# Halves on GpSimd, a ring for XW, and the roots, x's parts and row sums moved in a two-layer graph kernel

## The reference

```python
N, D = 2708, 128                      # nodes, features; adj is a 0/1 matrix
# layer 0
deg = jnp.clip(adj.sum(axis=1), 1.0);  dis = deg ** (-0.5)
diffusion = (dis[:, None] * adj * dis[None, :]) @ x - x
sim = x @ x.T / (norms[:, None] * norms[None, :])
attn = softmax(beta * sim * adj, axis=1)
x = layernorm(x + diffusion + sigmoid(alpha) * (attn @ x - x))
# layer 1
XW = x @ W;  s_col = XW @ a[0, :D];  s_row = XW @ a[0, D:]
den = exp(leaky_relu(s_row[:, None] + s_col[None, :], 0.01))
num = adj @ den
att = where(num != 0, den / num, 0.0)
out = layernorm(x + adj @ (att @ XW))
```

## Time and profile before

| | us |
|---|---|
| median of 3 runs (lowest, highest) | 685.43 (684.15, 686.16) |
| profiled execution, its own time | 685.51 |
| span of the profiled execution | 683.7 |
| busy in the span: PE, DVE, POOL, ACT | 575.0, 549.3, 428.3, 351.4 |

### The profile page before, as it was taken

One profiled execution on the slowest core, in us unless ns is written; L12 is line 12 of the kernel. 1 busy time (PEld: TensorE's weight loads), 2 busy tenths in 40 slices (PEclk: granted clock), 3 DMA queues, 4 the chain that ended last, 5 costly groups with the idle time before them and its releaser, 6 DMA issues.

```text
span 683.7 us, 11037 instructions
## 1 busy us (share of the span) xinstructions
PE 575.0 (84%) x4123; PEld 356.0 (52%) x4123; DVE 549.3 (80%) x1000; ACT 351.4 (51%) x556; POOL 428.3 (63%) x448
## 2 busy tenths in 40 slices
PE   0389999999998879999529987889989988848993
PEld 0245545555452868888518643334444443427883
DVE  1669999999997763678796877899998999985442
ACT  2335444444443513679977137777867877711000
POOL 5849999999999033455305176775777676003663
PEclk9999999999999589999757999999999999997998
DMA  9999890000000000000000031333333332000110
GB/s 146 104 108 108 143 376 3 1 0 1 1 1 3 4 0 16 25 16 18 16 1 24 18 113 46 93 89 86 90 90 90 86 82 81 1 5 9 32 29 16
DMA packets 17793, 37.17 MB, mean 54 GB/s; under 512 B 2570, under 2 KB 8222, under 8 KB 17726
## 3 DMA queue, kind: packets, MB, share of 16 engines
q0 software_dynamic: 7392, 24.32, 19.8%
q1 hardware_dynamic: 10334, 11.98, 5.4%
HBM read 48.72 MB, written 10.45 MB: 87 GB/s over the span
## 4 chain that ended last, share of the span: by engine, by line
PE 41%; POOL 22%; DVE 21%; ACT 8%; issue 5%; DMA 1%; DVEq 0%; POOLq 0%; ACTq 0%; SPq 0%
POOL R L403 21%; PE PSALL L1706 8%; PE PSALL L1604 7%; PE PSALL L1419 6%; DVE ring L1233 4%; PE PSALL L1665 4%; PE PSALL L1533 3%; ACT AW L590 3%; DVE ring L1226 3%; PE PSALL L1345 2%; PE PSALL L1612 2%; ACT R L687 2%; DVE FR L1233 2%; PE PSALL L1478 1%; PE PSALL L1442 1%
## 5 line engine op out<-in xcount | busy, mean ns | idle before, releaser
L403 POOL TENSOR_TENSOR R<-R,ring 128x452 f32<-128x452 f32 (+1 forms) x126 | 170.3, 1388 | 2.4 <-ACT ring L531 2.4
L531 ACT ACTIVATE ring<-ring,sm 128x452 f32<-128x452 f32 (+1 forms) x132 | 84.8, 667 | 102.9 <-DVE ring L836 102.7
L841 DVE TENSOR_TENSOR R<-ring 128x452 bf16<-128x452 f32 (+1 forms) x88 | 106.1, 1206 | 0.0
L1345 PE MATMUL PSALL<-XN 128*128 128x452 f16 (+2 forms) x396 | 99.2, 362 | 4.2 <-issue 4.2
L461 POOL DMA_INDIRECT AW<-ATd,FR x44 | 63.8, 1451 | 61.3 <-PE PSALL L1612 36.2
L1604 PE MATMUL PSALL<-AW,R 128*128 128x452 fp8e4 (+1 forms) x348 | 77.6, 354 | 24.9 <-DVE R L1165 18.6
L836 DVE TENSOR_TENSOR ring<-PSALL,AT 128x452 f32<-128x452 f32 (+1 forms) x132 | 78.6, 616 | 4.7 <-PE PSALL L1345 4.3
L1665 PE MATMUL PSALL<-ring,X 128*128 128x452 bf16 (+1 forms) x300 | 67.8, 360 | 0.9 <-DVE ring L1233 0.9
L1345 PEld LDWEIGHTS PSALL<-XN 128*128 128x128 f16 (+1 forms) x396 | 37.6, 98 | 56.7 <-issue 25.1
L1604 PEld LDWEIGHTS PSALL<-AW,R 128*128 128x128 bf16 x348 | 31.9, 97 | 64.6 <-DVE R L1165 26.8
L1233 DVE TENSOR_TENSOR ring<-ring 128x904 bf16<-128x904 f32 (+1 forms) x50 | 62.5, 1250 | 0.0
(11 more groups left out here) (252 smaller groups left out, 1083.5 us busy)
## 6 DMA issues: line engine op xcount, KB each, us to landing
AT<-in_adjT POOLq DMA_DIRECT2D x22, 338.5 KB, 26.4
ATd<-AT SPq DMA_DIRECT2D x2, 3723.5 KB, 16.8
XWd<-ring SPq DMA_DIRECT2D x11, 128.0 KB, 1.8
out<-ring SPq DMA_DIRECT2D x21, 64.0 KB, 1.5
AW<-ATd,FR POOLq DMA_INDIRECT x44, 4.3
X<-XWd,idx POOLq DMA_INDIRECT x22, 3.1
Wt<-in_W SPq DMA_DIRECT2D x1, 64.0 KB, 11.2
X<-in_x SPq DMA_DIRECT2D x1, 0.5 KB, 8.0
```

Source lines behind the costliest of these rows:

```text
L403: i = G.tensor_tensor(ES_, ES_, z, ALU.add)
L531: S.activation(z, z, ACT.Exp, scale=bcol[0:rows, :]).then_inc(s_exp, 1)
L841: V.tensor_tensor(Fl[q % 6][0:rows, 0:w], ring[0:rows, q % 6, 0:w], upper(q, rows, w), ALU.subtract).then_inc(s_low, 1)
L1345: m = TE.matmul(PSALL[0:rows, b, 0:w], lh[:, jt * P:jt * P + rows], rh[:, c0:c0 + w], start=(k == 0), stop=(k == 2))
```

## The change

- **Roots.** POOL's power is gone. ACT takes Ln and Exp of the degrees in the last tile of the attention, and DVE refines the result with five instructions on 22 columns (`roots`), behind the unit NU-4.
- **Parts of x.** DVE scales x in the last units (`scaled`, four instructions), ACT makes the high halves behind its last exponential, and DVE makes the low halves (`scaled_low`), three before the copies of `AOT` and one behind them. The float32 work of 12 instructions in four groups behind the copies is gone.
- **Row sums.** POOL splits all of `ES` (128 partitions by 2708) into 16-bit `ESh` and `ESl` behind its last addition, with one cast and one subtraction. PE sums them with 44 one-column matmuls of bfloat16, behind `spread(0)` and the first eight transposes. POOL's zeros for the pad come behind the two long instructions, and PE waits for them at the last group alone.
- **Loop.** POOL makes the halves of the gathered tiles (one tile for kind 0, two for kind 1), between `fetch_rows` and `fetch_xw`, with a register load of the kind and a branch. XW's halves go to a ring of four (`XW2`), two instructions instead of three. DVE and ACT also load the kind and leave out the second gathered tile for kind 0; DVE keeps the table's half (`sums_half`).
- `Fl` moves to another tensor; PE's general branch is rewritten, and is not the one that runs here.

```diff
+        XW2 = sb("XW2", [P, 4, 2, D], BF16)
...
-        Fl = [R1[:, 3 * NP + q * RW // 2:3 * NP + (q + 1) * RW // 2].bitcast(BF16) for q in range(6)]
...
+        Fl = [AWflat[:, q * RW:(q + 1) * RW] for q in range(6)]
+        ESh, ESl = XN[:, 0:NP // 2].bitcast(BF16)[:, 0:N], XN[:, NP // 2:NP].bitcast(BF16)[:, 0:N]
...
-                        gp.wait_ge(s_degmax, 1)
-                        G.tensor_tensor(dis, dis, mhalf.broadcast_to([P, T]), ALU.pow)
                     gp.wait_ge(s_exp, u + 1)
...
+            gp.wait_ge(s_esum, NU)
+            gp.wait_ge(s_logit, NU)
+            G.tensor_copy(ESh, ES[:, 0:N]).then_inc(s_es, 1)
+            gp.wait_ge(s_es, 1)
+            G.tensor_tensor(ESl, ES[:, 0:N], ESh, ALU.subtract).then_inc(s_es, 1)
             gp.wait_ge(s_aotA, 3)
             gp.wait_ge(s_aotD, 3)
-            gp.wait_ge(s_esum, NU)
...
-                gp.wait_ge(s_ohl[0], T)
-                gp.wait_ge(s_perm[0], 1)
                 gp.wait_ge(s_AT[t], 32)
-                if t:
-                    gp.wait_ge(s_xws, 3 * t)
-                G.tensor_copy(iota[:, :], XWs[:, t, :]).then_inc(s_xws, 1)
-                gp.wait_ge(s_xws, 3 * t + 1)
-                G.tensor_tensor(XWh[:, t, :, 0], XWs[:, t, :], iota[:, :], ALU.subtract).then_inc(s_xws, 1)
-                gp.wait_ge(s_xws, 3 * t + 2)
-                G.tensor_copy(XWh[:, t, :, 1], iota[:, :]).then_inc(s_xws, 1)
+                if t >= 4:
+                    gp.wait_ge(s_y, 3 * (t - 3))
+                G.tensor_copy(XW2[:, t % 4, 1, :], XWs[:, t, :]).then_inc(s_xws, 1)
+                gp.wait_ge(s_xws, 2 * t + 1)
+                G.tensor_tensor(XW2[:, t % 4, 0, :], XWs[:, t, :], XW2[:, t % 4, 1, :], ALU.subtract).then_inc(s_xws, 1)
...
-            for jt in range(2, T):
-                if jt + 4 < T:
-                    fetch_xw(jt + 4)
-                split_xw(jt)
-                fetch_rows(jt)
+
+            def halves(jt):
+
+                s = T + jt % 2 * DS
+                kind = eng.value_load(win[0:1, jt:jt + 1], min_val=0, max_val=2)
+                gp.wait_ge(s_dene, jt + 1)
+                met = gp.covered()
+                with eng.If(kind == 1):
+                    G.tensor_tensor(den_h[:, s + 1:s + DS, :, 0], den_w[:, s + 1:s + DS, :], den_h[:, s + 1:s + DS, :, 1],
+                                    ALU.subtract).then_inc(s_denb, 1)
+                gp.only(met)
+                with eng.Else():
+                    G.tensor_tensor(den_h[:, s + 1, :, 0], den_w[:, s + 1, :], den_h[:, s + 1, :, 1], ALU.subtract).then_inc(s_denb, 1)
+                gp.only(met)
+
+            def layer1(general):
+
+                for jt in range(2, T):
+                    fetch_rows(jt)
+                    if not general:
+                        halves(jt - 1)
+                    if jt + 4 < T:
+                        fetch_xw(jt + 4)
+                    split_xw(jt)
+                if not general:
+                    halves(T - 1)
...
                         S.activation(z, z, ACT.Exp, scale=bcol[0:rows, :]).then_inc(s_exp, 1)
+                    if (jt, c) == (T - 1, 1):
+                        av.wait_ge(s_dis, 1)
+                        S.activation(dup, dis, ACT.Ln).then_inc(s_dis, 1)
+                        av.wait_ge(s_dis, 2)
+                        S.activation(root0, dup, ACT.Exp, scale=-0.5).then_inc(s_dis, 1)
+                for k, (t0, nt) in enumerate(SL):
+                    av.wait_ge(s_xd, k + 1)
+                    S.activation(xp[:, t0:t0 + nt, 0, :], xd3[:, t0:t0 + nt, :], ACT.Copy).then_inc(s_xphi, 1)
...
+                kind = eng.value_load(win[0:1, jt:jt + 1], min_val=0, max_val=2)
                 av.wait_ge(s_denz, 3 * (jt + 1))
                 s = T + jt % 2 * DS
-                S.activation(den_w[:, s:s + DS, :], den_w[:, s:s + DS, :], ACT.Exp).then_inc(s_dene, 1)
+                met = av.covered()
+                with eng.If(kind == 1):
+                    S.activation(den_w[:, s + 2, :], den_w[:, s + 2, :], ACT.Exp)
+                av.only(met)
+                S.activation(den_w[:, s:s + 2, :], den_w[:, s:s + 2, :], ACT.Exp).then_inc(s_dene, 1)
...
+            def roots():
+
+                dv.wait_ge(s_dis, 3)
+                dv.wait_ge(s_up, 1)
+                k = own.step(V.tensor_tensor(cs, root0, root0, ALU.mult))
+                dv.wait_ge(own.sem, k)
+                k = own.step(V.tensor_tensor(cs, cs, dis, ALU.mult))
+                dv.wait_ge(own.sem, k)
+                k = own.step(V.tensor_scalar(cs, cs, -0.5, 1.5, ALU.mult, ALU.add))
+                dv.wait_ge(own.sem, k)
+                k = own.step(V.tensor_tensor(dis, root0, cs, ALU.mult))
+                dv.wait_ge(own.sem, k)
+                k = own.step(V.tensor_scalar(dup, dis, up_x, None, ALU.mult))
+                dv.wait_ge(own.sem, k)
+
+            def scaled(k):
+
+                t0, nt = SL[k]
+                V.tensor_tensor(xd3[:, t0:t0 + nt, :], X3[:, t0:t0 + nt, :],
+                                dup[:, t0:t0 + nt].unsqueeze(2).broadcast_to([P, nt, D]), ALU.mult).then_inc(s_xd, 1)
+
+            def scaled_low(k):
+
+                t0, nt = SL[k]
+                dv.wait_ge(s_xphi, k + 1)
+                V.tensor_tensor(xp[:, t0:t0 + nt, 1, :], xd3[:, t0:t0 + nt, :], xp[:, t0:t0 + nt, 0, :],
+                                ALU.subtract).then_inc(s_xp, 1)
...
+                    if not shifted:
+                        if u == NU - 4:
+                            roots()
+                        if NU - 4 < u <= NU:
+                            scaled(u - NU + 3)
+                        if u > NU:
+                            scaled_low(u - NU - 1)
...
                 dv.wait_ge(s_gather, NU)
                 for c in range(1, NC, 2):
                     c0, w = CH[c]
                     V.tensor_copy(AOT[:, c0:c0 + w], PSALL[:, c, 0:w]).then_inc(s_aotD, 1)
+                scaled_low(3)
...
-            for g, (t0, nt) in enumerate(SL):
-                V.tensor_tensor(xd3[:, t0:t0 + nt, :], X3[:, t0:t0 + nt, :],
-                                dis[:, t0:t0 + nt].unsqueeze(2).broadcast_to([P, nt, D]), ALU.mult).then_inc(s_xp, 1)
-                dv.wait_ge(s_xp, 3 * g + 1)
-                split2(xd3[:, t0:t0 + nt, :], xp[:, t0:t0 + nt], up_x, 3 * g + 2)
...
-            def small_scores(jt):
+            kinds = {}
+
+            def score(jt, q):
+
+                s = T + jt % 2 * DS
+                return V.tensor_scalar(den_w[:, s + 1 + q, :], cb3[:, jt, :], Rw[:, q, jt:jt + 1], r01w[:, q, jt:jt + 1],
+                                       ALU.add, ALU.max)
+
+            def small_scores(jt, usual):
 
                 s = T + jt % 2 * DS
                 if jt >= 2:
                     dv.wait_ge(s_num, 6 * (jt - 1))
                 dv.wait_ge(s_pick, 2 if jt < FIRST else 4)
+                if usual:
+                    kinds[jt] = eng.value_load(win[0:1, jt:jt + 1], min_val=0, max_val=2)
+                    met = dv.covered()
+                    with eng.If(kinds[jt] == 1):
+                        score(jt, 1)
+                    dv.only(met)
+                    score(jt, 0).then_inc(s_denz, 2)
+                else:
+                    for q in range(WN):
+                        score(jt, q).then_inc(s_denz, 1)
                 V.tensor_scalar(den_w[:, s, :], cb3[:, jt, :], e_bias[:, jt:jt + 1], e_cap, ALU.add, ALU.min).then_inc(s_denz, 1)
-                for q in range(WN):
-                    V.tensor_scalar(den_w[:, s + 1 + q, :], cb3[:, jt, :], Rw[:, q, jt:jt + 1], r01w[:, q, jt:jt + 1],
-                                    ALU.add, ALU.max).then_inc(s_denz, 1)
...
                                 ALU.subtract).then_inc(s_denb, 1)
+                sums_half(jt)
+
+            def sums_half(jt):
+
+                s = T + jt % 2 * DS
+                dv.wait_ge(s_dene, jt + 1)
                 V.tensor_tensor(den_h[LOROWS:P, s, :, 1], den_w[LOROWS:P, s, :], den_h[LOROWS:P, s, :, 1],
                                 ALU.subtract).then_inc(s_denb, 1)
...
                             if cp == 0:
-                                small_scores(jt + 1)
+                                small_scores(jt + 1, True)
                             if cp == 1:
-                                small_halves(jt + 1)
+                                sums_half(jt + 1)
...
+            def row_sums():
+
+                pe.wait_ge(s_es, 2)
+                for t in range(T):
+                    rows = rows_of(t)
+                    for k, part in enumerate((ESh, ESl)):
+                        m = TE.matmul(PSALL[0:rows, 5, t:t + 1], part[:, t * P:t * P + rows], ones[:, :],
+                                      start=(k == 0), stop=(k == 1))
+                m.then_inc(s_rsum, 1)
+                pe.wait_ge(s_wE, 1)
+                TE.matmul(PSALL[:, 4, 256:258], WTs, ac, start=True, stop=True).then_inc(s_wT, 1)
...
             for t in range(T):
```

(13 more changed lines are left out.)

83 lines of the change are left out of this document (45 added, 38 removed).

## The result

The changed kernel takes **675.5 us** (median of 4 runs, 674.03 to 677.47); the kernel before took 685.41 us on the same chip. The ratio is 0.9846, with a 95% interval of 0.9817 to 0.9874: it is faster by 1.5%. The profiled execution took 675.03 us with a span of 673.3 us, against 683.7 before. The forecast was 687.5 us, so it had the sign wrong, and its range (677 to 697) just missed the time.

A forecast was written before the change was run, and what follows sets the result against it. The prediction took VectorE to bound kind-0 loop tiles, TensorE kind-1 tiles, and row sums and first spreading to follow layer 0's attention; 7.7 us cost less 5.6 us gain, +2.1 on 685.43, gave 687.5 us, range 677 to 697.

The forecast's parts named there:

- turns of one each: Shared port: VectorE and GpSimd instructions alternate, nearly always one each; with this VectorE's copies of AOT end at 237.9 us.
- 7.7 us of cost: Transition to the spreading: attention rows start at 246.2 us instead of 238.53, carried on in full.
- The lower bound of the term: Transition cost: 5.8 us if the first spreading is at the full clock throughout.
- 5.6 us forecast: Loop, kind-0 tiles: a net gain of 0.40 us for each of 14 waits for VectorE.
- what comes back: Loop, kind-0 tiles: VectorE waits 0.36 us a tile for GpSimd's halves of one tile.
- the bounds, 0 to 10.4: Loop gain: 10.4 us if GpSimd's halves always fall in a VectorE gap, nothing if GpSimd is late.
- B: Rival, transition: VectorE keeps the port through its back-to-back run; cost 0.8 us, time 680.6 us; chance 0.16.
- its sign: Transition, mark of B in the trace: a GpSimd subtraction itself stretched to 9 us or more.
- my loop term: Loop: the gain of 5.6 us, 0.40 us for each of 14 waits at kind-0 tiles.
- C: Rival, transition: GpSimd's long cast and subtraction do not hold VectorE; rows 3.3 us earlier, time 676.5 us; chance 0.12.
- D: Rival, loop: GpSimd's halves come late or the register load is not hidden; 6.3 us slower, time 699.4 us; chance 0.12.
- the part on the shared reads: Port rule: VectorE instructions reading two SBUF tensors and GpSimd's reading any take turns; VectorE's PSUM readers are free.

The follow-up runs named there:

- e3: Changed kernel with each of VectorE's scaled and scaled_low waiting by semaphore for an earlier one, ten waits; 684.2 us, ratio 0.9979 to the kernel before.
- e9: Changed kernel with one wait added, of the first scaled_low for the last scaled; 682.9 us in one run.
- e15: Changed kernel with VectorE's copies of AOT behind the fourth scaled_low and no wait added; 676.2 us in one run.
- e11: The changed kernel run once more, unaltered, on another chip; 675.1 us, ratio 0.9859 to the kernel before.
- e7: Changed kernel with row sums still behind the first spreading but in float32 from ES, without GpSimd's cast and subtraction; 679.2 us, ratio 0.991 to the kernel before.
- e5: Changed kernel with the loop's halves of both tables back on VectorE; 679.7 us, ratio 0.9905 to the kernel before.
- e6: Changed kernel without kinds on ACT, GpSimd and VectorE: both tables in every tile, no register load for it; 680.6 us, ratio 0.9916 to the kernel before.
- e4: Changed kernel with XW's halves made by three GpSimd instructions in XWh, without the ring and its waits; 690.2 us, ratio 1.0051 to the kernel before.
- e13: Changed kernel with one wait added, of the second scaled_low for the first; 680.5 us in one run.
- e14: Changed kernel with one wait added, of the third scaled_low for the second; 678.4 us in one run.

## Why the prediction was wrong

**The transition: the order of the port, the step that failed.** The sum took turns of one each between the two engines, "in nearly every case one each", and put GpSimd's additions, cast and subtraction between VectorE's four lows, four `scaled` and three `scaled_low`. The rows it came from the earlier trace rows show GpSimd beside VectorE instructions of which the next was not yet ready, or beside PSUM readers: L474 asked at 454.10 while L1226 ran, and the exponential that L1233 waits for ended at 454.90. In the run of the changed kernel, where each instruction was ready before the one ahead ended, GpSimd waited. The copies came at 226.5 and not at 236.2, the cast and subtraction fell beside the copies and the first spreading, and 7.7 us of cost became a gain of 1.2 us at the rows. e3 shows that the rest of the working had the right shape but was some 3 us too long: with the gaps in, the copies end at 235.3 (237.9 forecast) and the rows start at 243.2 (246.2), 4.7 us later than in the kernel before and not 7.7. The cast started at 222.53 there, not at 224.5, and the last `scaled` and the first `scaled_low` were over before the subtraction held VectorE. I had the row that spoke for the other case in hand, the cast of 2.75 us at 420.54, and took it for an exception.

**Its sizes.** The cast was 2.4 us in the working: its end at 228.86 is 2.31 us behind the end of the held `scaled_low` at 226.55, and it was 2.73 us in e9. Subtraction 5.3: 5.32 in e15, 5.65 with a short wait. Row sums 1.3: 1.34. First spreading 4.3: 4.75, and 3.82 in e11. The lower bound of the term does not follow from its own numbers: half of 4.3 us off 7.7 gives 5.5, not 5.8; and the sum for the row sums is 245.2, not 245.3. Neither matters here. VectorE's last steps to the rows 0.9: 237.30 less 235.98, 1.3. The Trainium skill's rule of a lock held for the whole instruction ("SBUF — State Buffer", section "Who interferes with whom") says who is shut out, and L951's 5.42 us beside the subtraction agree with it. It also says that the engine that issues first gets the pair. This case's trace does not agree: the addition was ready at 220.83, and four VectorE instructions that started from 221.80 on went ahead of it. The order decided here, and for it the measurement counts.

**Something I left out of the sum was the clock of TensorE under the row sums.** I counted 8.90 us taken away and was right that 16-bit sums are 1.3, but e7 shows that 4.2 of the 8.90 went with the lower level at that place.

**The loop: 5.6 us forecast, 8.7 measured.** The term that was mis-sized is the one for what comes back, 0.36 us a tile for GpSimd's halves: it is 0.01 in the tile shown (0.45 less 0.44, e5) and 0.09 on average (0.45 less 0.36). The other terms hold: 0.45 for L1163, 0.25 for the second score (0.29 in the sum), next to nothing for the third XW instruction (0.02), register loads hidden (e6). The net is 0.62 us for each of the 14 waits instead of 0.40, 8.7 us. It lies inside the bounds, 0 to 10.4. That TensorE's own part is not the next bound was right: 0.60 to 1.11 us of waiting for VectorE were left at each of these tiles.

**The rivals.** B had the mechanism, at 0.16, though not its sign (a subtraction of GpSimd stretched to 9 us; it was the addition that stood, 4.90 us): copies 228.2 (229 there), subtraction ends 234.6 (236.5), rows 237.30 (239.3). It gave 680.6 us because it had 0.8 of cost where 1.2 was gained, and my loop term. With 8.7 for the loop and 1.2 of gain it is 675.5. C had the number, 676.5, and the wrong mechanism: long instructions of GpSimd do hold VectorE, L951 here and two `scaled_low` for 3 and 6 us in e3. D did not come, but e4 shows the part of it that concerns GpSimd's queue one small instruction away.

**What would have made it right** is to ask of each row, in the part on the shared reads, what VectorE had next in its queue at that moment and whether it was ready.

## What to carry to other kernels

A GpSimd instruction that needs the port it shares with VectorE was shut out here for the whole of a run of ready VectorE instructions, so work for GpSimd beside such a run starts near its end, and its cost is to be put beside what stands there; one harmless looking semaphore wait in the run turned this round and made the span up to 7.8 us longer (e9, 681.1 against 673.3 us, one run). Before work is moved to an engine off the critical path, count that engine's own tile with the longest durations its rows show: here the move of the halves is worth some 4 us (e5), and with GpSimd's third instruction for XW put back the kernel is slower than before (e4). When an operation on TensorE is costed at a place just behind an idle stretch, read the granted clock there: here its place behind other work gave as much as its smaller size.

## What the runs showed of the hardware that was not expected

- The last addition of GpSimd, 1.14 us of work, stood 4.90 us behind five ready VectorE instructions, and 5.78 us behind six in e15.
- One semaphore wait in VectorE's list moved the grant to an instruction ahead of it (held: the first `scaled_low` in e13, the second in e14, the low ahead of the last `scaled` in e9; one run each).
- A VectorE instruction with a single input of 22 columns, L951, was held for 5.42 us by GpSimd's subtraction; in e15 it was 0.63 us, held by the cast's end, and went ahead of the subtraction.
- GpSimd's indirect fetches, 0.94 us with VectorE quiet, took up to 1.84 us in the changed kernel's loop (562.15 us), 2.60 us in e4 (467.29 us) and 2.99 us in the loop of the kernel before (417.55 us).
- The same 44 float32 row sums took 8.90 us at a granted clock of 0.50 and 4.73 us at 1.00.
